# Delta rule: where ScalarE's copies of a chunk's outputs stand against the lower exponents two chunks ahead

## What is computed

```
x  = L0_attn_out;  xn = layernorm(x)
s  = delta rule(xn)                 # the part around the change
g  = silu(mixture of 8 experts(xn))
x  = x + s * g                      # then a second layer: state-space scan and ternary MLP

# delta rule, for each batch row and each of 2 heads, chunk by chunk:
cum    = cumsum(log_decay)
L_mask = tril(exp(cum[:, None] - cum[None, :]))
M      = tril(-(wk_scaled @ wk.T) * L_mask, -1)
A      = inverse(eye - M)
intra  = tril(rk @ wk.T * L_mask, -1)
v_new  = A @ v_scaled - A @ wk_scaled_dec @ S
o      = rk_decay @ S + intra @ v_new
S      = exp(cum[-1]) * S + wk_tail.T @ v_new
out    = xn + o @ W_read.T
```

## Time and profile before

| | us |
|---|---|
| median of 3 runs | 2408.51 (2408.32 to 2412.16) |
| the profiled execution's own time | 2399.99 |
| its span, first to last instruction | 2398.3 |

### The profile page before, as it was taken

The page is one execution under the profiler, slowest core; times in us unless marked ns, Lnnn a source line. Parts: engine busy times, 40 slices in busy tenths (PEclk is TensorE's granted clock), DMA queues, the critical chain, the costliest instruction groups (busy, mean ns, idle before and its releaser), DMA issues.

```text
span 2398.3 us, 36952 instructions
## 1 busy us (share of the span) xinstructions
PE 2197.5 (92%) x12464; PEld 1788.7 (75%) x12464; DVE 1843.5 (77%) x2832; ACT 1646.8 (69%) x2715; POOL 1449.4 (60%) x1026
## 2 busy tenths in 40 slices
PE   6799897999999999996999999999999999999986
PEld 4788796998898898884667667676676765776765
DVE  5574453667766666677989989989899899898995
ACT  6775542555555556666887788787877877888774
POOL 0236563111111113336988989889889898898895
PEclk8899998999999999997999999999999999999988
DMA  8434544566666654444655655555555555565563
GB/s 291 85 56 111 112 125 136 181 236 232 234 230 230 233 209 152 133 126 154 219 169 190 198 184 186 194 186 202 176 186 195 199 187 177 185 211 177 178 208 101
DMA packets 235434, 430.22 MB, mean 179 GB/s; under 512 B 35089, under 2 KB 117457, under 8 KB 235234
## 3 DMA queue, kind: packets, MB, share of 16 engines
q1 hardware_dynamic: 229090, 410.87, 53.0%
q0 software_dynamic: 6144, 16.79, 2.2%
HBM read 353.61 MB, written 73.96 MB: 178 GB/s over the span
## 4 chain that ended last, share of the span: by engine, by line
PE 54%; DVE 13%; issue 9%; ACT 9%; DMA 6%; POOL 6%; SPq 1%; another core or an unknown queue 1%; POOLq 1%; DVEq 0%; ACTq 0%
PE pb L1641 11%; PE pb L1614 11%; DVE pb L2094 6%; PE pb L2406 5%; PE pb L2411 5%; PE pb L994 3%; PE pb L2305 2%; PE pb L2432 2%; PE pb L2321 2%; DVE UU L2100 2%; DMA XB<-xnd 2%; PE pb L2330 2%; DMA CC<-bcd 2%; POOL UU L2019 2%; POOL UU L2027 1%
## 5 line engine op out<-in xcount | busy, mean ns | idle before, releaser
L2019 POOL TENSOR_TENSOR UU<-dx,BB 128x1024 f32<-128x1024 f32 x256 | 614.6, 2409 | 112.0 <-DMA BB<-bcd 83.6
L2231 ACT ACTIVATE pb<-dt,al 128x512 f32<-128x512 f32 x512 | 339.5, 685 | 149.4 <-DVE UU L2100 147.8
L2100 DVE TENSOR_TENSOR UU<-pb,CC 128x512 f32<-128x512 f32 x512 | 351.3, 686 | 24.3 <-DMA CC<-bcd 6.5
L2094 DVE TENSOR_TENSOR_SCAN pb<-pb,hs,UU 128x512 f32<-128x512 f32 x256 | 328.5, 1283 | 10.7 <-ACT pb L2231 7.4
L2094 DVE TENSOR_TENSOR_SCAN pb<-pb,UU 128x512 f32<-128x512 f32 x256 | 313.0, 1223 | 8.5 <-ACT pb L2231 7.9
L1381 POOL TENSOR_TENSOR clo_b<-craw_b,chi_b 128x1024 fp32r<-128x1024 f32 x22 | 62.3, 2830 | 405.9 <-ACT chi_b L1444 405.9
L1531 DVE TENSOR_TENSOR HL<-HF,HH 128x512 fp32r<-128x512 f32 x220 | 159.6, 728 | 179.9 <-ACT HH L1436 165.7
L2406 PE MATMUL pb<-HAh,WH 128*128 128x512 f32 x1024 | 282.7, 419 | 7.0 <-DVE dt L2075 5.1
L1431 ACT ACTIVATE HF<-pb,BU 128x512 f32<-128x512 f32 x192 | 132.3, 689 | 219.4 <-PE pb L1614 191.9
L2411 PE MATMUL pb<-HAl,WH 128*128 128x512 f32 x1024 | 259.7, 396 | 0.0
L1641 PE MATMUL pb<-W2h,HH 128*128 128x256 f32 x880 | 256.0, 291 | 1.0
(11 more groups left out here) (336 smaller groups left out, 4891.0 us busy)
## 6 DMA issues: line engine op xcount, KB each, us to landing
WH<-fhd SPq DMA_DIRECT2D x176, 512.0 KB, 3.5
BB<-bcd SPq DMA_DIRECT2D x256, 256.0 KB, 4.7
CC<-bcd SPq DMA_DIRECT2D x256, 256.0 KB, 5.0
raw<-in_w1a SPq DMA_DIRECT2D x23, 1024.0 KB, 7.3
raw<-in_w2a SPq DMA_DIRECT2D x23, 1024.0 KB, 7.4
craw_b<-in_fch SPq DMA_DIRECT2D x22, 512.0 KB, 5.9
fhd<-chi_b SPq DMA_DIRECT2D x22, 512.0 KB, 3.9
fld<-clo_b SPq DMA_DIRECT2D x22, 512.0 KB, 4.9
```

Source lines behind the costliest of these rows:

```text
L2019: e.tensor_tensor(ubuf(n)[:], dx[p][:], BB[n % 3][:].rearrange("p (a m) -> p a m", a=1).to_broadcast([P, 2, 512]), ALU.mult).then_inc(p_u. ...
L2094: e.tensor_tensor_scan(h_[:], h_[:], uu[:, c, :], first, ALU.mult, ALU.add).then_inc(v_sc.sem, 1)
L2100: e.tensor_tensor(uu[:, c, :], abank(n, c)[:], CC[n % 3][:], ALU.mult).then_inc(v_mu.sem, 1)
L2231: e.activation(abank(n, c)[:], dt[p][:, c, :], ACT.Exp, scale=al1[:, 2 * p + c, s:s + 1]).then_inc(c_a.sem, 1)
```

## The change

In `act_a` the two copies of chunk n's outputs to `OT` now stand directly behind the copies of the new values, and `lower(n + 2)` stands behind them. In the count of `g_act`'s steps `o` moves in the same way. Nothing is added or removed, and no wait changes; the transfers that SP issues are the same.

```diff
@@ -201,7 +201,7 @@
-                        ["d4", "wk", "rk''", "ETr'", "ET'", "t5", "ez'", "rc'", "rT''", "t6", "MT'", "vn", "Er''", "E''", "o"]) for h in range(2)]
+                        ["d4", "wk", "rk''", "ETr'", "ET'", "t5", "ez'", "rc'", "rT''", "t6", "MT'", "vn", "o", "Er''", "E''"]) for h in range(2)]
@@ -965,13 +965,13 @@
                 for m in range(0 if more else 2):
                     e.wait_ge(s_w0[m], 16)
                     e.activation(WB[0][2 * m][:], fview[m], ACT.Copy).then_inc(s_w0h, 1)
-                if n + 2 < NSEQ:
-                    lower(n + 2)
                 for h in range(2):
                     e.wait_ge(*g_pe[h].at("o", n))
                     if n:
                         e.wait_ge(s_y, 2 * n)
                     e.activation(OT[h][:], four(gbank("o", n, h)), ACT.Copy).then_inc(g_act[h].sem, 1)
+                if n + 2 < NSEQ:
+                    lower(n + 2)
                 if n + 3 < NSEQ:
                     for b in range(4):
                         squares((n + 3 + 8 * b,))
```

## The result

| | before | after |
|---|---|---|
| median of 21 runs each, one chip | 2407.68 us (2394.14 to 2412.16) | 2413.84 us (2403.8 to 2420.56) |
| span of the profiled execution | 2398.3 us | 2409.1 us |

The changed kernel is slower. The ratio is 1.0028, with a 95% interval of 1.0016 to 1.0040, which is 6.7 us (3.9 to 9.6); the two medians themselves differ by 6.16 us. The forecast was 2415.3 us, or 6.81 us more.

The account below looks back on a forecast made before the run. PE, busy 2197.5 us, was taken as the bound, so only its idle time could move. The terms 3.39 + 1.09 + 2.33 = 6.81 us, set on the median of 2408.51, gave 2415.3 us, range 2408.0 to 2420.0.

Parts of the forecast that it names:

- The delay of the squares: ACT at a chunk's end: squares start 4.09 us after PE's `S` of head 1, in chunk 1 3.39 us later.
- Chunk 0 into 1: Head of chunk 1: squares start 1.09 us later, and with no cover PE loses all 1.09 us.
- Chunk 1 into 2: Head of chunk 2: squares start 3.39 us later, and with no cover PE loses all 3.39 us.
- The clock: PE, `D4` to `D5` of chunk 2: after a 4.76 us wait a slower TensorE clock costs 2.33 us (bounds 0 and 2.33).
- Chunks 2 to 4: Heads of chunks 3 and 4: pauses cover the late squares, cost 0, at most 5.38 us together.
- Chunk 4: Chunk 4 into 5: squares not late, `y` 1.82 us earlier, gain runs into a pause; 0, at least -1.82 us.
- the clock stays up: Rival, chunk 2: same delays without the clock's 2.33 us, +4.48 us, 2413.0 us; chance 0.18.
- The delay is covered: Rival: pauses at the heads of chunks 3, 4 and 5 swallow the earlier loss, 2409.3 us; chance 0.18.
- the later chunks pay too: Rival: pauses ride along with DVE, up to 5.38 us on top, 12.19 us in all, 2420.7 us; chance 0.12.
- the second pause vanishes: Rival: earlier `y` in chunk 4 removes the 8.95 us pause, -3.96 us, or -6.29 without the clock term; chance 0.08.

Follow-up runs that it names:

- r5: Changed kernel with chunk n+3's squares and root moved directly behind the copies of the new values: 2405.35 us against 2408.05 for the kernel before, ratio 0.9988.
- r3: Kernel before with the copies moved ahead of `lower` in chunk 1 alone: 2406.97 us against 2402.14, ratio 1.002 (1.0003 to 1.0036).
- r2: Changed kernel again, unaltered, for one more profile: 250.64 us from chunk 0 to 6, against 249.32 in its first profile.
- r9: Changed kernel again, unaltered, timed and profiled on a third chip: 2364.93 us against 2359.75 for the kernel before, ratio 1.0029.
- r7: Changed kernel with 32 unused transposes on PE between `P4` and `D4` of chunk 2, filling the wait: chunk 1 to 2 40.61 us, whole kernel 2413.6 us.
- r8: Kernel before with the copies moved ahead of `lower` in chunks 2 to 5 alone, third chip: 2359.23 us against 2359.75, ratio 0.9999.
- r1: Kernel before again, unaltered, for one more profile: 246.58 us from chunk 0 to 6, against 241.54 in its first profile.
- r4: Kernel before with the copies moved ahead of `lower` in chunk 4 alone: 2401.94 us against 2402.14, ratio 0.9996 (0.9981 to 1.001).
- r11: Kernel before a third time, unaltered, for its profile on a fourth chip: chunk 1 to 2 38.54 us, chunk 0 to 6 243.20 us.
- r10: r5 with one router part (three DVE instructions) moved behind chunk 2's `Pm`, third chip: 2354.44 us against 2359.75 for the kernel before, ratio 0.9984.

## Why the prediction was right

It named the direction, the way through the square root, and 6.81 us against a measured 6.7 (3.9 to 9.6). Its parts did less well than the sum.

- **The delay of the squares: right.** They start 4.07 us behind PE's `S` of head 1, where the rule said 4.09. DVE's `rn` waited 4.28 us, where 0.91 + 3.39 = 4.30 was named. That the loss goes through the square root is shown by r5, where it disappears.
- **Chunk 0 into 1: right for the execution it was read from.** 1.09 us were forecast and 1.09 measured between the two profiles. Over all profiles the new order of chunk 0 takes 39.18 to 39.20 us and the old one 37.39 to 38.20 (six profiles, 37.8 in the mean), so the term is 1.0 to 1.8 us, 1.4 in the mean. That the one profile hit it to a hundredth is luck.
- **Chunk 1 into 2: right in kind, a little too large.** Of the 3.39 us, 3.15 reached `D4`, and so 0.24 were absorbed. The forecast took DVE to run from `rn` to `Pm` without a gap. There was a small one: from `rn` to `Pm` it took 168.30 - 159.46 = 8.84 us before and 171.30 - 162.67 = 8.63 after. The second `M` waits some 0.2 us for PE's `kk` when the root is in time, as r5's rows show, and no longer when it is late.
- **The clock: the mis-sized step.** The forecast computed a wait of 4.76 us and took the price of chunk 3's wait, 2.33 us. The wait was 4.37, because of the 0.24 us absorbed and because `P4` itself came 0.64 us later and not 0.49: PE's `wkS` had to wait 0.41 us for the bank that DVE's `XS` frees, and `XS` stands behind `norms` too. This was a second queue behind the same late root, which the forecast had not followed. The price was 1.01 us in three profiles and 1.87 in r3, and nowhere 2.33. PE did not come back slow, as it had in chunk 3, where the clock was 0.50 from the start of `D4` at 210.25 until 216.5. In the changed kernel the clock was 1.00 at the start of `D4`; it fell 0.6 us later (0.8 in r2 and r9), and the 16 products took 3.25 us and not 3.8. Only in r3 had it fallen ahead of `D4`. And the old order of chunk 1 pays 1.01 in two profiles of five. Over the profiles in the table the new order of chunk 1 (four profiles, without r7) pays (3 x 1.01 + 1.87) / 4 = 1.2 us and the old order 2 x 1.01 / 5 = 0.4. The change adds about 0.8 us by the clock, where 2.33 were in the sum.
- **Chunks 2 to 4: right as 0, the reason only in part.** The forecast let the pauses cover the delay. At chunk 3 one does end `Pm`'s wait in the changed kernel as well, but it did not shrink (3.56 us, where it was 3.51), and its end moved with the late start, by 4.75 us. What shrank was DVE's wait ahead of the second `M`, from 2.54 to 0.52 us. And r8 shows that without any pause PE does not wait for `Pm` either: no part of the router stands between `norms` and `Pm`, and a cover of that size was there all the time. The forecast mentions the missing router part in half a sentence and gives the cover to the pause. What the late start does on a chip with the pauses was not timed by itself: there the whole loss of 6.7 us (3.9 to 9.6), less 5.4 for chunks 0 and 1 (below), leaves 1.3 us (-1.5 to 4.2) for them.
- **Chunk 4: not decided.** PE's `y` no longer waits, as named, but the 1.82 us were those of one execution, and so was the late landing of `ZR` on which "they are not late" rested; r1 has neither. r4 can't tell the mean worth from zero.

The terms that are measured make 1.4 + 3.15 + 0.8 = 5.4 us. The timed loss is 6.7 (3.9 to 9.6), and 6.8 (4.0 to 9.7) on the other chip, where the medians differ by 5.18. The rest is inside the interval, and where it comes from, if it exists, stays open. So the sum was close because a clock term that was 1.5 us too large made up for a chunk 0 that was 0.3 too small and for what may be scatter; that part was luck.

"TensorE: Matmul & The Clock Gate" in the Trainium skill, section "HAM oscillation — how this bites in real kernels", says that a TensorE left waiting between bursts starts the next one throttled, and pays each time. Behind the long wait of chunk 2 (4.36 to 4.37 us) the traces agree that it pays: all four profiles did, and in r7, with the wait filled, the clock stayed at 1.00 and some 1.05 us were gone. They agree on the start only in r3; in the other three the burst began at 1.00. Behind the short wait (1.86 to 1.88 us) two of seven profiles paid, r8 and r11, and five did not.

Of the rivals, "the clock stays up" (+4.48 us) lies in the interval as well. Its sum is nearer to the 5.4 us of the measured terms, though its statement is wrong: the clock did fall in all three profiles of the changed kernel. "The delay is covered" (+0.8 us), "the later chunks pay too" (+12.19) and "the second pause vanishes" (-6.29) lie outside the interval of 3.9 to 9.6. The first of these named what decides it, an end of the pause that stays where it is, and the end moved.

## What to carry to other kernels

On an engine that works in order, a copy which waits should not be moved ahead of work that could run during that wait, unless something else fills it: here `lower` ran free of charge in ACT's 4.76 us of idle time, and moved behind the wait it delayed the square root, for which DVE and then PE waited. Ask first what stands behind the moved instruction in its list and who waits for the last of it; the right filler is the short work whose result is due soonest (r5), and the work that nobody waits for goes last. Here a delay cost PE nearly all of its length only in the bodies in which the engine between had no slack, so look for the bodies with extra work in them (the router's, in chunks 1 and 2), and remove that work from the path too (r10).

## What was not expected of the hardware

- The clock can fall behind a short wait. r11 waited 1.88 us and had a mean granted clock of 0.68 over the next 4 us; the first profile waited 1.86 us and had 1.00 over 168 to 176 us. A wait of 4.36 to 4.37 us cost 1.01 us in three profiles and 1.87 in one. It is a price with a scatter, and not a fixed step. Nor need the clock be low when the work begins again: behind the 4.37 us it was 1.00 at first and fell 0.6 us into the work.
- The chip of r8 to r10 was 2% faster with the same program: 2359.75 us against 2402.14 to 2408.05. The pauses that no engine ends were absent at the heads of its chunks 3 to 6. The stretch from chunk 0 to 6 took 224.47 us against 249.32 and 250.64 with the changed kernel. Windows over the same work of the same program, from `S` in chunk 2 to `S` in chunk 6 of the changed kernel, r9 and then r2:

```profile
196.06:339.69 143.63, 140.03 (x1210) 133.74 (x1209) 77.94 (x174) 90.97 (x239) 100.37 (x177) 1.00 0.55 127
```

```profile
196.36:366.08 169.72, 145.41 (x1211) 138.52 (x1209) 78.43 (x174) 91.47 (x239) 102.97 (x188) 0.94 0.44 108
```

PE is idle for 3.6 of 143.63 us in the one and for 24.3 of 169.72 us in the other. What the pauses wait for was not tried and stays open. They are far larger than the change studied here, and differ between chips, so times are compared only within one chip.
